# Two graph-attention layers with a layer norm on one core: ScalarE's order in a step, and GpSimd's second subtraction behind a tile's first weighing

## What is computed

```python
def _gat_layer(x, W, adj):
    proj = x @ W
    Wh, Ws = jnp.split(proj, 2, axis=-1)
    scores = Wh @ Ws.T
    a = jax.nn.softmax(scores, axis=-1) * adj
    out = a @ Wh
    out = out + x
    return jax.nn.leaky_relu(out, 0.01)

y = _gat_layer(_gat_layer(x, W_stack[0], adj), W_stack[1], adj)
return _layernorm(x + y, axis=-1)
```

## Time and profile before

| | |
|---|---|
| median of 3 runs | 1680.99 us (1677.59 to 1681.62) |
| profiled execution | 1675.62 us, span 1673.7 us, 23474 instructions |
| TensorE busy | 1588.3 us, 95% of the span |
| VectorE busy | 1233.2 us, 74% |
| GpSimd busy | 917.6 us, 55% |
| ScalarE busy | 678.8 us, 41% |
| granted clock of TensorE | 0.99 of full speed |
| DMA | 302.59 MB, mean 181 GB/s |
| chain that ended last | PE 55%, DVE 22%, ACT's queue 7%, POOL 6%, ACT 5%, issue 3% |

### The profile page before, as it was taken

The page is one execution under the profiler, slowest core; times in us unless marked ns, Lnnn a source line. Parts: engine busy times, 40 slices in busy tenths (PEclk is TensorE's granted clock), DMA queues, the critical chain, the costliest instruction groups (busy, mean ns, idle before and its releaser), DMA issues.

```text
span 1673.7 us, 23474 instructions
## 1 busy us (share of the span) xinstructions
PE 1588.3 (95%) x8104; PEld 1319.3 (79%) x8104; DVE 1233.2 (74%) x1558; ACT 678.8 (41%) x1175; POOL 917.6 (55%) x935
## 2 busy tenths in 40 slices
PE   7899999999999999999788999999999999999996
PEld 6778888888788888887677888888788888877885
DVE  4567777777777777777636788778878888787785
ACT  4333444444434444444333444344434444434442
POOL 2355555555555555555444555555555555555565
PEclk9999999999999999999999999999999999999998
DMA  5357767777767776768913777777677777777774
GB/s 182 86 147 185 193 185 184 186 198 182 184 186 192 184 186 187 195 186 220 261 32 105 193 192 184 192 201 194 177 191 202 196 186 189 197 190 185 199 192 126
DMA packets 167750, 302.59 MB, mean 181 GB/s; under 512 B 39760, under 2 KB 68432, under 8 KB 167504
## 3 DMA queue, kind: packets, MB, share of 16 engines
q1 hardware_dynamic: 105808, 132.75, 32.3%
q0 software_dynamic: 36864, 134.23, 27.6%
q10 hardware_dynamic: 24960, 34.11, 8.4%
HBM read 157.29 MB, written 9.44 MB: 100 GB/s over the span
## 4 chain that ended last, share of the span: by engine, by line
PE 55%; DVE 22%; ACTq 7%; POOL 6%; ACT 5%; issue 3%; DMA 1%; SPq 0%; POOLq 0%
PE banks L443 18%; PE banks L336 9%; PE banks L338 9%; PE banks L337 9%; PE banks L445 9%; DVE neg_max L641 8%; DVE ring L669 7%; ACTq L242 7%; POOL a_lo L766 6%; DVE ring L674 4%; ACT a_hi L559 3%; ACT ring L540 1%; DMA turned<-ring 1%; DVE weight L660 1%; DVE wh L605 1%
## 5 line engine op out<-in xcount | busy, mean ns | idle before, releaser
L766 POOL TENSOR_TENSOR a_lo<-turned,a_hi 128x512 fp32r<-128x512 f32 x512 | 718.4, 1419 | 667.3 <-ACT a_hi L559 666.8
L443 PE MATMUL banks<-wh,a_hi 128*128 128x512 f32 x2048 | 753.6, 406 | 50.7 <-POOL a_lo L766 43.2
L540 ACT ACTIVATE ring<-banks,neg_max 128x1024 f32<-128x1024 f32 x256 | 286.0, 1117 | 815.2 <-DVE neg_max L641 815.2
L445 PE MATMUL banks<-wh,a_lo 128*128 128x256 f32 x2048 | 577.5, 282 | 0.0
L443 PEld LDWEIGHTS banks<-wh,a_hi 128*128 128x128 f32 x2048 | 387.9, 189 | 182.6 <-POOL a_lo L766 83.0
L641 DVE TENSOR_REDUCE neg_max<-banks 128x1 f32<-128x1024 f32 x256 | 310.9, 1214 | 261.8 <-PE banks L338 261.8
L336 PE MATMUL banks<-x_t,q_t 128*128 128x512 f32 x1024 | 405.8, 396 | 4.0 <-DVE x_t L605 2.4
L338 PE MATMUL banks<-x_t,q_t 128*128 128x512 f32 x1024 | 401.8, 392 | 0.0
L337 PE MATMUL banks<-x_t,q_t 128*128 128x512 f32 x1024 | 400.9, 391 | 0.0
L445 PEld LDWEIGHTS banks<-wh,a_lo 128*128 128x128 f32 x2048 | 390.0, 190 | 5.8
L669 DVE SCALAR_TENSOR_TENSOR ring<-ring,weight,load 128x1024 f32<-128x1024 f32 x256 | 377.0, 1472 | 7.3 <-DMA load<-adj 4.6
(11 more groups left out here) (68 smaller groups left out, 729.6 us busy)
## 6 DMA issues: line engine op xcount, KB each, us to landing
load<-adj POOLq DMA_DIRECT2D x256, 512.0 KB, 5.0
turned<-ring SPq DMA_DIRECT2D x1528, 64.0 KB, 4.0
turned<-ring ACTq DMA_DIRECT2D x520, 64.0 KB, 4.0
ring<-x SPq DMA_DIRECT2D x8, 512.0 KB, 5.0
rows<-x SPq DMA_DIRECT2D x32, 128.0 KB, 4.3
x_scratch<-rows SPq DMA_DIRECT2D x32, 128.0 KB, 3.9
rows<-x_scratch SPq DMA_DIRECT2D x32, 128.0 KB, 4.3
first_rows<-x SPq DMA_DIRECT2D x32, 128.0 KB, 4.0
```

The source lines that it names most:

```text
L443: nc.tensor.matmul(psum[:, bank, :], a_hi[:, s, b], wh[:, k].rearrange("p a d -> p (a d)"), start=start, stop=stop, skip_group_check=True)
L445: last = nc.tensor.matmul(psum[:, bank, 0:D], a_lo[:, s, b], wh[:, k, 0], start=False, stop=stop, skip_group_check=True)
L540: nc.scalar.activation(ring[:, i % RING, :].rearrange("p (b e) -> p b e", b=2), psum[:, 2 * (i % 2):2 * (i % 2) + 2, :], ACT.Exp, bias=neg ...
L766: nc.gpsimd.tensor_tensor(a_lo[:, j % 2].rearrange("p b (r j) -> p b r j", r=QUADS), as_f32(turned[:, unit % 2, :, b:b + SUB, :]).rearrang ...
```

## The change

Three things. ScalarE's order in a step becomes: first split, factor of the tile whose fourth chunk was in the step before (now a function of its own, `chunk_factors`), second split, moves of chunk s - 4, exponentials of chunk s. `row_weights` multiplies and sums in one operation, so it has three instructions and no longer four. And in each step in which a tile's first chunk is weighed, GpSimd's second subtraction waits until that weighing is done.

```diff
--- before.py
+++ after.py
-        STAT_STEPS = 4
+        STAT_STEPS = 3
...
-                if c == CPT - 1:
-                    all_of = slice(t % 2 * CPT, (t % 2 + 1) * CPT)
-                    act.wait_ge(row_max_done, t + 1)
-                    nc.scalar.activation(factor[:, all_of], neg_max[:, all_of], ACT.Exp,
-                                         bias=row_neg_max[:, t % 2:t % 2 + 1], scale=-1.0).then_inc(factor_done, 1)
+
+            def chunk_factors(t):
+                all_of = slice(t % 2 * CPT, (t % 2 + 1) * CPT)
+                act.wait_ge(row_max_done, t + 1)
+                nc.scalar.activation(factor[:, all_of], neg_max[:, all_of], ACT.Exp,
+                                     bias=row_neg_max[:, t % 2:t % 2 + 1], scale=-1.0).then_inc(factor_done, 1)
...
             for step in range(STEPS):
-                k = chunk_at(step - LAG_PRODUCT)
+                k, summed = chunk_at(step - LAG_PRODUCT), tile_at(step - CPT)
                 if k is not None:
                     split_a(2 * k)
+                if summed is not None:
+                    chunk_factors(summed)
+                if k is not None:
                     split_a(2 * k + 1)
+                for m in weighed_at(step):
+                    if not is_drained(m):
+                        move_blocks(m)
...
                 if i is not None:
                     exponentials(i)
-                for m in weighed_at(step):
-                    if not is_drained(m):
-                        move_blocks(m)
...
                 dve.wait_ge(factor_done, t + 1)
-                nc.vector.tensor_tensor(scaled_sum[:, of], factor[:, of], chunk_sum[:, of],
-                                        ALU.mult).then_inc(stat_step, 1)
+                nc.vector.scalar_tensor_tensor(scaled_sum[:, of], factor[:, of], 1.0, chunk_sum[:, of], ALU.mult, ALU.mult,
+                                               accum_out=row_sum[:, p:p + 1]).then_inc(stat_step, 1)
                 dve.wait_ge(stat_step, done + 1)
-                nc.vector.tensor_reduce(row_sum[:, p:p + 1], scaled_sum[:, of], AXIS_X, ALU.add).then_inc(stat_step, 1)
+                nc.vector.reciprocal(row_inv[:, p:p + 1], row_sum[:, p:p + 1]).then_inc(stat_step, 1)
                 dve.wait_ge(stat_step, done + 2)
-                nc.vector.reciprocal(row_inv[:, p:p + 1], row_sum[:, p:p + 1]).then_inc(stat_step, 1)
-                dve.wait_ge(stat_step, done + 3)
...
                 pool.wait_ge(hi_done, j + 1)
+                m = j // 2 + LAG_PRODUCT - LAG_WEIGH
+                if j % 2 and m % CPT == 0 and m // CHUNKS == j // 2 // CHUNKS:
+
+                    pool.wait_ge(a_done, m + 1)
```

## The result

The changed kernel takes 1719.3 us (median of 4 runs, 1711.75 to 1722.47), the kernel before 1680 us (median of 4, timed in turns with it). The ratio is 1.0224, with a 95% interval of 1.0198 to 1.0251: **slower by 2.2%**, some 38 us by the ratio and 39 by the medians. Forecast were 1714 us and slower.

The account below looks back on a forecast made before the run. TensorE, 95% busy, was taken as the bound, waiting on a four-engine chain before one product. That product, 0.56 us later a tile times 59, gives 33 us: 1681 + 33 = 1714 us, range 1676 to 1742.

Parts of the forecast that it names:

- the new first operation ends with the subtraction: VectorE's multiply-and-sum, two SBUF inputs, starts 0.12 us after GpSimd's first subtraction and stands until that ends, 4.39 after the maximum's start.
- the faster rival: VectorE's small operations pass despite starting 0.12 us after the subtraction; 0.26 us a tile won, 1666 us; chance 0.14.
- Read-out of the sum: VectorE's cost for handing out the multiply-and-sum's total: 0.10 us taken, bounds nothing or 0.20.
- Two issues: ScalarE's two move issues ahead of the exponentials of a tile's first chunk: 1.25 us, bounds 1.17 and 1.65.
- c0: Step after a tile's fourth-chunk maximum: the next tile's first chunk is scored, this tile's first chunk weighed.
- The signal to GpSimd: Price of GpSimd's second subtraction waiting for the weighing's end: a signal of 0.08 us.
- product of c1: TensorE's product one step after the first chunk's weighing; forecast 12.27 us after the fourth-chunk maximum's start, against 11.71 before.
- GpSimd's wait: GpSimd's second subtraction waits for the first chunk's weighing, keeping 1.28 us off the path.
- Moves ahead: ScalarE's moves before exponentials: the split follows the exponentials' start by 1.10 us, not 1.43; hidden outside the first-chunk step.
- c3: Third step after the one weighing a tile's first chunk; its moves were forecast hidden in a longer TensorE gap.
- Count of tiles: 118 TensorE waits for GpSimd's subtraction, two a tile, give 59 of 64 tiles, each losing 0.56 us.
- The two rows for a small operation that stands: VectorE rows as evidence: 128x4 weight operation at 1465.52 took 1.29 us, line 705's 128x1 addition 0.933, beside a subtraction.

Follow-up runs that it names:

- the fused one: Kernel before with only the fused multiply-and-sum, three small VectorE operations for four: 1661.97 us, ratio 0.9902.
- the faster version: Kernel before plus fused multiply-and-sum, odd chunks' moves ahead of ScalarE's exponentials, SyncE making all eight moves of a tile's first chunk: 1648.56 us, ratio 0.982.

## Why the prediction was right

The sign and most of the size came from one step, "the new first operation ends with the subtraction", and that step is shown: by the trace after, by putting the factor back (31 of the 38 us gone), and by the operation with one input, which passes in the same place. The chance of 0.14 for the faster rival hung on whether a start 0.12 behind the subtraction could pass; it never did.

- *Read-out of the sum:* 0.10 taken, and it is cheaper: the reciprocal starts at +4.43 and not +4.52. It is an instruction of its own (0.08 at 534.24), nearly all of it before the operation's own end at 534.31. The Trainium skill's count of two instructions (VectorE: DVE Perf Modes, Two Vector instructions with no wait between them) holds in this trace, but the bound of 0.20 that the prediction put on it was not reached.
- *Two issues:* 1.25 taken, 1.40 measured. ScalarE and SyncE released at the same instant do cost, 0.23 over the 1.17 of before, short of the bound of 0.48. The kernel before has it too: in 10 turns both began together in c0, and ScalarE's two issues took 1.38 to 1.40.
- *The signal to GpSimd:* 0.08 taken, and 0.15 measured, from the weighing's end at +6.17 to the second subtraction at +6.32. Read-out 0.09 less, signal 0.07 more, issues 0.15 more, and some hundredths elsewhere make the 0.07 by which the product of c1 comes later than forecast.
- *GpSimd's wait:* right that it costs nothing by itself (the run with it alone) and that the change needs it (the run without).
- *Moves ahead:* the split 1.10 behind the exponentials came, at 1.11. But I booked no effect of the moves in c3 on their own; what they do there, making the first split 0.16 sooner, is 0.16 us that costs 70 us or nothing, by what it meets. In the change it was worth its own size: with the moves behind, all of c0 came 0.17 later.
- *Count of tiles:* 59 forecast, 62 found, and that 118/2 came so near was luck. In the kernel before 48 tiles have two waits for GpSimd, 11 have one, and the last tile of each layer has 4 and 7. In 12 tiles ScalarE's two issues of c3 took 1.35 to 2.27 us and not 1.16, so the subtraction came late and the weighing went first. Ten of the 12 were 0.1 us faster than the others, and they too are slow now. So 62 x 0.6 = 37 us, against 36 between the two profiled executions and 38 by the ratio.
- *The two rows for a small operation that stands:* only the addition of line 705 has two tensor inputs. The weight operation of 1465.52 has one and a pointer; it stood as well, but it shows nothing of two tensor inputs. The step was right, on one fitting row and not two.

Left open: that the changed kernel's runs lie 7 to 11 us above its profiled one (1711.75), while those of before stay within 6 of theirs (1675.62); none of the traces shows where.

## What to carry to other kernels

On VectorE a tiny operation is not cheap if it has two SBUF inputs and a GpSimd operation on SBUF has just begun: here it waited for all of it, 1.18 us instead of 0.17. Before an operation is moved earlier on a third engine, look at what it makes coincide; here 0.16 us on ScalarE was worth 4.2% the wrong way. The order to aim for is a chain of small operations that is over before the partner's long one begins, and the fewer of them the easier it is.

## What the runs showed of the hardware

- **Who starts first, and by how much.** Between a VectorE operation and GpSimd's subtraction the gap of their recorded starts decides. The weighing passed at leads of 0.08 us and more in the kernel before and 0.07 and more in the fused one. At a lead of 0.05 (808.22 against 808.27) it stood, and in the run with GpSimd's wait alone one passed with as much, while 0.03 stood. So the border lies at about 0.05, and GpSimd may start later by the record and still be first. The weight operation passed at 0.17, once at 0.06 (in the faster version), and stood at 0.00 (543.23 on both). The turn with the lead of 0.05, VectorE of the kernel before and then GpSimd:

```profile
808.22 2.39 DVE L669 SCALAR_TENSOR_TENSOR ring<-ring,weight,load 128x1024 f32<-128x1024 f32 x1
```

```profile
808.27 3.48 POOL L766 TENSOR_TENSOR a_lo<-turned,a_hi 128x512 fp32r<-128x512 f32 x2 [2.55 <-ACT a_hi L559]
```

- **TensorE's clock.** In the run without GpSimd's wait TensorE's weight loads stood 2.2 us in every tile, and 19 of 59 tiles then had some 3.5 us at the lower level (mean clock 0.93 against 1.00). In the run with the moves ahead alone they stood 2.1 us, and only 2 of 59 tiles did: those from 764.77 and from 1402.90, 27.56 and 26.16 us long at 0.94 and 0.93. The others without side work stayed at 24.3 us and 1.00. What tells them apart wasn't tried.
